# Last stage of a four-stage transformer kernel: load order, the engine that zeroes the key tiles, and the order of items within a slot

## The reference, cut to what matters

```
x = x + layer1(layer0(layernorm(x)))            # two layers, each:
h = shift_token(x); q, k, v = split(h @ wqkv)    # 8 heads of 64
q = l2norm(q) * q_scale;  k = l2norm(k) * k_scale
q, k = rotary_xpos(q, k)                         # cos and sin tables, one per position
o = softmax(8 q k^T, masked to a window of 64 back) @ v
x = x + o @ wo
h = layernorm(shift_token(x)) * g + b
a, g = split(h @ w1 + b1);  x = x + (a * gelu(g)) @ w2 + b2   # hidden width 341
```

## Time and profile before

| | us |
|---|---|
| median of 3 runs | 2061.22 |
| the profiled execution's own time | 2058.43 |
| its span on the core | 2056.5 |
| last stage, first load issued to last store issued | 1551.24 to 2050.97 |
| busy over the whole span: PE, DVE, ACT, POOL | 1762.6, 1661.3, 1602.7, 1224.6 |

### The profile page before, as it was taken

How to read it: one execution, slowest core, us unless ns; L and a number is a source line. 1 busy time by engine, 2 the same in 40 slices (tenths; PEclk the granted TensorE clock), 3 DMA queues, 4 the chain that set the end, 5 groups by cost and what they waited for, 6 DMA issues and landing times. The chain is left out here.

```text
span 2056.5 us, 37700 instructions
## 1 busy us (share of the span) xinstructions
PE 1762.6 (86%) x9830; PEld 1327.8 (65%) x9830; DVE 1661.3 (81%) x4303; ACT 1602.7 (78%) x5245; POOL 1224.6 (60%) x2106
## 2 busy tenths in 40 slices
PE   1788998899899889989989588669994999999996
PEld 0566776677677667767767456246562777777775
DVE  3799999999999999999998432768885788777784
ACT  1798999898899999999998223489971788888884
POOL 1267776777677677677777433359884555454450
PEclk8899999999999999999999699779997999999998
DMA  2222122122212222222220321012212000000000
GB/s 79 74 76 78 73 88 77 68 80 85 73 70 89 72 75 80 84 74 74 90 75 22 112 74 43 18 62 103 93 72 79 1 1 1 1 1 2 1 1 21
DMA packets 75299, 120.50 MB, mean 59 GB/s; under 512 B 10536, under 2 KB 59952, under 8 KB 67872
## 3 DMA queue, kind: packets, MB, share of 16 engines
q1 hardware_dynamic: 65920, 109.91, 15.3%
q10 hardware_dynamic: 7920, 5.60, 1.0%
q0 software_dynamic: 1248, 2.59, 0.4%
HBM read 95.44 MB, written 24.20 MB: 58 GB/s over the span
## 5 line engine op out<-in xcount | busy, mean ns | idle before, releaser
L436 ACT ACTIVATE a_prob<-a_scores,a_negmax 128x256 f32<-128x256 f32 x1536 | 706.5, 484 | 85.3 <-DVE a_negmax L538 57.9
L538 DVE TENSOR_REDUCE a_negmax<-a_scores 128x2 f32<-128x512 f32 x768 | 518.3, 675 | 43.5 <-PE a_scores L672 43.0
L684 PE MATMUL a_heads<-a_prob,a_diag 128*128 128x256 f32 x1920 | 478.2, 389 | 40.6 <-POOL a_diag L327 40.6
L327 POOL TENSOR_TENSOR a_diag<-ident,a_rowinv 128x256 f32<-128x256 f32 (+1 forms) x384 | 280.2, 735 | 248.7 <-DVE a_rowinv L592 243.5
L684 PEld LDWEIGHTS a_heads<-a_prob,a_diag 128*128 128x128 f32 x1920 | 358.3, 195 | 96.7 <-POOL a_diag L327 51.6
L672 PE MATMUL a_scores<-a_spread,a_spread 72*128 72x256 bf16 x1536 | 265.0, 276 | 92.9 <-ACT a_prob L436 53.9
L436 ACT ACTIVATION_READ_ACCUMULATOR a_prob<-a_scores,a_negmax 128x1 f32 x1536 | 330.9, 215 | 0.0
L672 PEld LDWEIGHTS a_scores<-a_spread,a_spread 72*128 72x128 bf16 x1536 | 127.6, 98 | 213.1 <-ACT a_prob L436 102.7
L1477 DVE TENSOR_TENSOR_SCAN c_state<-c_decay,c_psD 128x1024 f32<-128x1024 f32 x64 | 146.1, 2286 | 35.8 <-PE c_psD L1594 26.5
L1309 POOL TENSOR_TENSOR c_du<-c_state,c_c_row 128x1024 f32<-128x1024 f32 x64 | 151.3, 2365 | 30.3 <-DVE c_state L1477 21.2
L1933 ACT ACTIVATE d_prob<-d_psS,d_bias 128x128 f32<-128x128 f32 (+1 forms) x256 | 99.0, 396 | 35.5 <-DVE d_bias L2064 34.6
(11 more groups left out here) (291 smaller groups left out, 4111.4 us busy)
## 6 DMA issues: line engine op xcount, KB each, us to landing
a_spread<-a_split SPq DMA_DIRECT2D x48, 576.0 KB
a_spread<-a_split SPq DMA_DIRECT2D x144, 192.0 KB
a_split<-a_parts SPq DMA_DIRECT2D x48, 384.0 KB
c_c_row<-c_rows SPq DMA_DIRECT2D x32, 512.0 KB, 3.6
b_w<-in_b_w SPq DMA_DIRECT2D x1, 2816.0 KB, 14.9
a_w<-in_a_w ACTq DMA_DIRECT2D x10, 256.0 KB, 5.4
b_w<-in_b_w SPq DMA_DIRECT2D x1, 1536.0 KB, 17.9
d_wqkv<-in_d_wqkv SPq DMA_DIRECT2D x2, 768.0 KB, 5.8
```

Source lines behind the costliest of these rows:

```text
L327: g.tensor_tensor(diag[part % RING][:], ident[:].unsqueeze(1).broadcast_to([P, len(heads), P]), rowinv[part % RING][:, heads.start:heads.s ...
L436: ins = a.activation(prob[part % RING][:, c, :], psS[part % 2][:, c, :], ACT.Exp, bias=negmax[part % 2][:, c:c + 1], accum_out=rowsum[part ...
L538: v.tensor_reduce(negmax[part % 2][:, hs], psS[part % 2][:, hs, :], AX.X, ALU.max, negate=True).then_inc(s["negmax_ready"], 1)
L684: ins = p.matmul(psH[:, t, :], diag[part % RING][:, k, :], prob[part % RING][:, c, :], start=(j == 0 and k == 0), stop=(j == HG - 1 and c ...
```

## The change

Three edits. The loads are issued in another order: wqkv of layer 0, tables and both gains first, on a semaphore `first_in`, then mask and down, then the rest; PE and POOL begin on `first_in` (and `const_in`), and the rest (`weights_in`) is awaited by ACT ahead of the first exp and by PE ahead of the first turn_p. The four zero fills of kT go from DVE to POOL, two ahead of each of POOL's two first powers, and DVE waits for rot ahead of each projection instead of once. In `schedule_d` several items get other slots (shift, norm_f, turn_f, hidden and out_f one later; turn_h one later; the projections and turn_qk in other rows), and `rank` sorts a slot otherwise: hidden comes right behind exp and ahead of score, norm_f ahead of turn_p, shift behind turn_p, and turn_h, norm_o and out_f are ranked too.

```diff
--- before.py
+++ after.py
@@ -1701,22 +1701,23 @@
             place(last + 3, ("norm_o", q, t))
             place(last + 4, ("turn_o", q, t))
             place(last + 5, ("out_o", q, t))
-        place(at + 15, ("shift", q))
+        place(at + 16, ("shift", q))
         place(at + 16, ("rstd_f", q))
-        place(at + 16, ("norm_f", q))
-        place(at + 17, ("turn_f", q))
-        place(at + 22, *[("hidden", q, f) for f in range(NFD - 1)])
-        place(at + 24, ("hidden", q, NFD - 1))
-        place(at + 25, ("out_f", q))
+        place(at + 17, ("norm_f", q))
+        place(at + 18, ("turn_f", q))
+        for f, n in enumerate((23, 23, 25)):
+            place(at + n, ("hidden", q, f))
+        place(at + 26, ("out_f", q))
     for q in range(UNITS):
-        at = 8 * (q - 1)
-        place(at, ("turn_h", q))
-        for t in range(TPS):
-            for part in range(3):
-                place(at + 2 + 3 * t + part, ("project", q, t, part))
-            for part, n in enumerate(((4, 6), (6, 10))[t]):
+        at = 8 * q - 8
+        place(at + 1, ("turn_h", q))
+        for t, rows in enumerate(((1, 2, 2), (4, 5, 9))):
+            for part, n in enumerate(rows):
+                place(at + n, ("project", q, t, part))
+        for t, rows in enumerate(((5, 5), (6, 9))):
+            for part, n in enumerate(rows):
                 place(at + n, ("turn_qk", q, t, part))
-    rank = ('score', 'exp', 'shift', 'turn_o', 'turn_p', 'out_o', 'pv', 'hidden')
+    rank = ('exp', 'hidden', 'score', 'norm_f', 'turn_p', 'shift', 'turn_o', 'pv', 'out_o', 'turn_h', 'norm_o', 'out_f')
     order = []
     for n in sorted(slots):
         order += sorted(slots[n], key=lambda i: rank.index(i[0]) if i[0] in rank else len(rank))
@@ -1769,7 +1770,7 @@
         psO = ctx.enter_context(nc.psum_tensor("d_psO", [P, GRP], F32))
         psW = ctx.enter_context(nc.psum_tensor("d_psW", [P, GRP], F32))
 
-        names = ("const_in", "weights_in", "chain", "var_ready", "rstd_ready", "y_ready", "set_up",
+        names = ("const_in", "first_in", "weights_in", "chain", "var_ready", "rstd_ready", "y_ready", "set_up",
                  "rot_ready", "q_full", "q_free", "s_full", "s_free", "t_full", "t_free", "w_full", "w_free",
                  "o_full", "o_free", "square_ready", "rope_ready", "ss_ready", "inv_ready", "qk_ready", "pool_step",
                  "bias_ready", "rowinv_ready", "hn_ready",
@@ -1833,12 +1834,16 @@
         with nc.Block() as block:
             @block.sync
             def _(sp):
-                for dst, name in ((tables, "d_tables"), (mask, "d_mask"), (down, "d_down")):
+                sp.dma_start(wqkv[0][:], d["d_wqkv"][0]).then_inc(s["first_in"], 16)
+                sp.dma_start(tables[:], d["d_tables"]).then_inc(s["first_in"], 16)
+                for l in range(DEPTH):
+                    sp.dma_start(gains[l][:], d["d_gains"][l]).then_inc(s["first_in"], 16)
+                for dst, name in ((mask, "d_mask"), (down, "d_down")):
                     sp.dma_start(dst[:], d[name]).then_inc(s["const_in"], 16)
-
                 for l in range(DEPTH):
-                    for dst, name in ((wqkv, "d_wqkv"), (wo, "d_wo"), (w1, "d_w1"), (w2, "d_w2"), (cols, "d_cols"),
-                                      (gains, "d_gains")):
+                    if l:
+                        sp.dma_start(wqkv[l][:], d["d_wqkv"][l]).then_inc(s["weights_in"], 16)
+                    for dst, name in ((wo, "d_wo"), (w1, "d_w1"), (w2, "d_w2"), (cols, "d_cols")):
                         sp.dma_start(dst[l][:], d[name][l]).then_inc(s["weights_in"], 16)
 
             @block.gpsimd
@@ -1853,12 +1858,17 @@
                     g.wait_ge(s["set_up"], 2 * u + 2)
                     g.memset(prob[1][u][:, :, 0:WINDOW], 0.0).then_inc(s["set_up"], 1)
                 for k in range(2):
+                    g.wait_ge(s["set_up"], 5 + 2 * k)
+                    if k:
+                        g.wait_ge(s["rstd_ready"], k)
+                    g.memset(kT[k][P // 2:P, :, 0, :], 0.0).then_inc(s["set_up"], 1)
+                    g.wait_ge(s["set_up"], 6 + 2 * k)
+                    g.memset(kT[k][0:P // 2, :, 1, :], 0.0).then_inc(s["set_up"], 1)
                     g.wait_ge(s["var_ready"], k + 1)
                     g.tensor_tensor(mb[k]["rstd"][:], mb[k]["var"][:], minus_half[:, 0:H2], ALU.pow)\
                         .then_inc(s["rstd_ready"], 1)
-                g.wait_ge(s["set_up"], 5)
-                g.wait_ge(s["const_in"], 48)
-                g.wait_ge(s["weights_in"], DEPTH * 6 * 16)
+                g.wait_ge(s["set_up"], 9)
+                g.wait_ge(s["first_in"], (2 + DEPTH) * 16)
                 for l in range(DEPTH):
                     for k in range(4):
                         g.tensor_tensor(rot[l][:, k], tables[:, k],
@@ -1904,8 +1914,7 @@
             def _(a):
                 a.sem_inc(s["t_free"], SL)
                 a.sem_inc(s["s_free"], SL)
-                a.wait_ge(s["set_up"], 5)
-                a.wait_ge(s["weights_in"], DEPTH * 6 * 16)
+                a.wait_ge(s["set_up"], 9)
 
                 def full(it):
                     n = TI[it]
@@ -1957,6 +1966,8 @@
                             a.activation(kT[q % 2][lo, :, 0, ts], turned_in[lo], ACT.Copy)
                             a.activation(kT[q % 2][hi, :, 1, ts], turned_in[hi], ACT.Copy).then_inc(s["t_free"], 1)
                     elif kind == "exp":
+                        if it == ("exp", 0, 0):
+                            a.wait_ge(s["weights_in"], (DEPTH * 5 - 1) * 16)
                         exps(it)
                     elif kind == "turn_p":
                         t = heads(it[2])[0]
@@ -2003,12 +2014,7 @@
                                               ALU.subtract, ALU.mult)
                 chain.link(ins)
                 v.sem_inc(s["y_ready"], 1)
-                v.wait_ge(s["const_in"], 48)
-                for u in range(2):
-                    v.memset(kT[u][P // 2:P, :, 0, :], 0.0)
-                    chain.link(v.memset(kT[u][0:P // 2, :, 1, :], 0.0))
-                v.sem_inc(s["y_ready"], 1)
-                v.wait_ge(s["rot_ready"], DEPTH * 4)
+                v.wait_ge(s["const_in"], 32)
 
                 def heads3(ap):
                     return ap.rearrange("p (h e) -> p h e", e=DHD)
@@ -2019,6 +2025,7 @@
                         _, q, t, part = it
                         i = Q[it]
                         ps = psQ[i % 2]
+                        v.wait_ge(s["rot_ready"], (q // SEQS + 1) * 4)
                         v.wait_ge(s["q_full"], i + 1)
                         if part == 2:
 
@@ -2121,10 +2128,10 @@
             @block.tensor
             def _(p):
                 p.sem_inc(s["t_full"], SL)
-                p.wait_ge(s["y_ready"], 2)
-                p.wait_ge(s["const_in"], 48)
-                p.wait_ge(s["set_up"], 5)
-                p.wait_ge(s["weights_in"], DEPTH * 6 * 16)
+                p.wait_ge(s["y_ready"], 1)
+                p.wait_ge(s["const_in"], 32)
+                p.wait_ge(s["set_up"], 9)
+                p.wait_ge(s["first_in"], (2 + DEPTH) * 16)
 
 
                 def bank(it):
@@ -2172,6 +2179,8 @@
                         p.matmul(out, qT[q % 2][:, c, t * P:(t + 1) * P], kT[q % 2][:, c, :, k0:k1], start=True,
                                  stop=True).then_inc(s["s_full"], 1)
                     elif kind == "turn_p":
+                        if it == ("turn_p", 0, 0):
+                            p.wait_ge(s["weights_in"], (DEPTH * 5 - 1) * 16)
                         g = it[2]
                         t = heads(g)[0]
                         p.wait_ge(s["s_free"], S[("score", q, g)] + 1 + SL)
```

## The result

Before: 2061.18 us, median of 20 runs (2054.19 to 2068.46). After: **2073.52 us**, median of 20 (2059.61 to 2081.15). The ratio of the two is 1.0057, 95% interval 1.0041 to 1.0072: slower, by about 12 us. It lies within the range and on the side that had the largest chance, but it is twice the +6.0 of the sum.

What follows compares the result with a forecast made beforehand. PE bounded the old stage, a ring of dependencies the new repeat; -3.6 (start) - 3.6 (first unit) - 1.0 (end) + 1.1 + 13.1 (repeats) = +6.0 us on 2061.2 gave 2067.2 us, range 2050 to 2078.

Steps and rivals of the forecast that it cites:

- The repeat: Steady stretch between hidden(q,2) items on PE: 29.26 us instead of 28.17, over 12 repeats +13.1 us; chance 0.50.
- the ring: Chain of in-order and data dependencies from hidden(q,2) through PE, ACT and DVE to the next unit's: at least 29.26 us.
- PE's floor: Rival for the repeat: PE stays the bound and loses both waits, 27.17 us a repeat, total 2040; chance 0.10.
- the repeat as before: Rival: items slide past the supposed ring, the repeat stays 28.17 and only the ends change, -8.2 us, 2053; chance 0.20.
- The longer ring through psW: Rival: out_o waits for DVE's copy of shift to free psW; repeat 30.0 us, +15.7, total 2077; chance 0.12.
- The wait for rot ahead of each projection is always met: nothing.: Start step: DVE's wait for rot, now ahead of each projection, costs no time.
- nothing but the order can make a repeat longer: Bounding step: no engine gets more work, so only the order lengthens a repeat; gain at most 1.0 us a repeat.
- the first term: First unit: DVE begins the second tile's projection before the first turn_qk, saving 3.6 us, bounds 0 and 5.
- I give them half each: The two units before the 12 whole repeats, with only part of the hidden items: half a repeat's loss each, +1.1 us.
- The start: Stage start: fills on POOL and reordered loads let PE begin earlier, saving 3.6 us, bounds 1.0 and 4.5.
- My rival: Stage start: DVE's writing of y holds up POOL's fills, 1.7 us saved instead of 3.6, total 2069; chance 0.08.
- The end: Last pv and norm_o go ahead of out_f and turn_f: 2.5 us instead of 3.48, saving 1.0, bounds 0 and 2.5.

Runs made afterwards that it cites:

- the copy on and off the ring: Kernel after plus one needless 512-column DVE copy, behind the first tile's value copy (on) or norm_o (off): 2084.52 us on, 2079.83 off.
- The version above: Against before: new loads, fills on ACT, rot behind y, its wait once a layer, old order except unit 0's second tile, out_f(13), turn_f(14): 2055.36 us, ratio 0.9955.

## Why the prediction was right, and where it was not

**The repeat: right, with two legs off that cancel.** 29.26 summed, 29.22 measured with the order alone. Of the seven legs five are within 0.12 us. DVE's from the projection to the exp was 0.42 too long in the sum, and PE's from turn_p to the mark 0.55 too short. That the sum came within 0.04 us is thus partly luck. The waits named for PE (0.9 ahead of turn_p, 0.3 or more ahead of s5, none for L2112) all stand in the trace, and the copy on and off the ring shows that it is the ring that decides, more clearly still once the clock's share of the long repeats is known. PE's floor (27.17) and the repeat as before (28.17) are out. The longer ring through psW was partly right: its wait is there in each repeat (L2218, 3.2 us in 12, mostly 0.24), so the ring does close through DVE's copy of shift; its price was too high, 0.24 instead of 0.74.

**"The wait for rot ahead of each projection is always met: nothing."** This step failed. It costs 0.21 us in a new repeat and 0.14 in an old one (28.31 against 28.17), and 0.2 to 0.4 us between the fifth score and the first hidden item. Together these are some 2.8 us, a third of the 8.5 that the sum missed in the stage. So "nothing but the order can make a repeat longer" was wrong too. A met wait is no stall, but here it lengthens each hand-over behind it.

**The units ahead of the first hidden item: the term of the largest error, 5.8 us.** I had -3.6 and +1.1; measured is +3.28. Measured in two parts it is -1.95 up to unit 0's fifth score on DVE (31.40 us behind PE's start against 33.35) and +5.23 from there to the first hidden(·,2) (68.24 against 63.01). Timeline of DVE in the first unit:

```profile
1581.43 0.69 DVE L2041 TENSOR_TENSOR d_direct<-d_psQ,d_rot 128x512 f32<-128x512 f32 x1 [0.63 <-POOL d_qk L1902]
...
1592.08 0.69 DVE L2041 TENSOR_TENSOR d_direct<-d_psQ,d_rot 128x512 f32<-128x512 f32 x1 [5.78 <-ACT d_sq L1929]
```

The second tile's projection starts 13.84 us behind PE's start, where 13.8 was predicted (17.3 before), and DVE's 3.66 us of idle are gone from there. But DVE then idles 5.78 us until 1592.08, ahead of unit 1's first projection, and from 1587.70 on PE runs at 0.50. In the kernel with one rot wait a layer, where PE had 0.50 for 7.3 us less, the fifth score comes 3.24 us earlier than before (30.11), and nearly all of the predicted 3.6 is there. So the first term was near right, and some 1.3 us of it went with the clock, which differs from trace to trace.

**"I give them half each", +1.1: this is the step that failed by the most.** The same stretch behind the fifth score, at full clock in every trace, takes 67.75 us with the order alone and 68.08 with one rot wait a layer, 4.7 and 5.1 more than before. These units lack the hidden items, but may not lack the ring's other legs; that reason is mine and untested. No row stood behind the half. The version above, with the old order, has 63.03 there, and its first hidden item at 92.45, 3.9 earlier than before; some of the 3.9 may be the clock as well, at 0.50 for 12.0 us of this piece against 17.4.

**The start: 2.76 of 3.6.** The size of a fill was right (0.95 and 0.94 us, 0.91 predicted), and so was what the halves would do but for one: the loads alone cost 1.7. What was missing is who holds whom. Timeline of after:

```profile
1560.39 0.95 POOL L1864 MEMSET d_kT<- 64x1024 f32 x1
...
1560.93 0.43 DVE L69 TENSOR_SCALAR d_m_mean<-d_m_sm 128x8 f32<-128x8 f32 x1
1561.39 0.94 POOL L1866 MEMSET d_kT<- 64x1024 f32 x1
1561.40 0.97 DVE L70 TENSOR_SCALAR d_m_var<-d_m_dd 128x8 f32<-128x8 f32 x1
1561.48 5.99 DVE L2012 TENSOR_SCALAR d_y_tok<-x_tok,d_m_mean,d_m_rstd 128x128 f32<-128x128 f32 x16
...
1564.05 3.34 POOL L1874 TENSOR_TENSOR d_rot<-d_tables,d_gains 128x128 f32<-128x128 f32 x8
```

POOL's fills keep their length, and DVE's TENSOR_SCALAR of 8 elements a lane, 0.17 us elsewhere, takes 0.43 and 0.97 and ends with the fill. The same holds beside rot: y took 5.99 us for 16 tiles against 4.79 with rot behind it, and even this is 0.6 more than without fills: the first tile takes 0.95 us, until the fourth fill ends, and the ninth waits for POOL's second power. My rival had the contention, but the wrong way round (DVE holding POOL) and at the wrong instruction. The Trainium skill, "SBUF — State Buffer", section Who interferes with whom, says that a VectorE instruction in a 2-port mode and GpSimd block each other for a whole instruction: by the 0.97, which begins 0.01 us behind the fill, the trace agrees. Here the GpSimd instruction is a fill, which only writes. The BATCH_NORM_STATS2 beside the first pair of fills kept its 1.6 us.

**The end: right in kind.** From the last pv at 2044.33 to turn_o at 2046.89 it took 2.56 us, 2.5 predicted, 3.48 before. The tail as a whole bears it out between these two traces, with 1.56: both have 6.8 us at a clock of 0.50 in it, behind this place. Against other traces it can't be compared: fills alone, with the old order throughout, has 47.71 where before has 50.09, and only 2.8 us at 0.50.

**The sum.** -2.76 + 3.28 + 15.53 - 1.56 = +14.5 in the profiled executions, +12 by the medians, +6.0 predicted. The terms missed by 0.8, 5.8, 2.4 and -0.6. Of the repeats' 2.4 too many, 2.0 are the rot wait (12 x 0.17 above 29.26), the rest one repeat of 29.80.

**Open.** What lowers the clock inside the repeats of two traces (order alone, copy beside the ring) and not in the others, no run tells; each such stretch of 3.4 us cost 1.7 us. In the 29.80 of after one score on DVE (L2071, at 1782.63) starts 0.35 us late, and three other traces have one or two such starts, at other instructions; the cause is open. How the 4.7 to 5.1 us that the new order costs in the first three units are spread over its items was not taken apart either.

## What to carry to other kernels

In a software-pipelined order no engine need be the bound: follow one item through every in-order queue and back to itself, with distances between starts from the trace, and compare the sum with the busiest engine; here a copy on that ring cost its length and the same copy beside it almost nothing, and the next ring was only some tenths away. Put a wait that is needed once where it is needed once. When work is moved to an idle engine, look at what its neighbour does in the same microseconds, and price the filling of the pipeline by its own rows, not as a share of the steady state. Before a difference between two traces is put down to an edit, lay the granted clock of the same stretch side by side.

## What the runs showed of the hardware that was not expected

- A semaphore wait on DVE that is always met adds 0.11 us to each hand-over from ACT that follows it (0.80 instead of 0.69 from start to start).
- The granted clock can fall to 0.50 for 3.4 us in the middle of a steady stretch in one execution: in the order alone at 1909.50 us, with the copy beside the ring twice, each time as out_o began, and it cost 1.7 us each time. Ahead of the first hidden item, 16.7 instead of 9.4 us at 0.50 went with 1.3 us.
- A POOL fill of 64x1024 f32 holds a small DVE TENSOR_SCALAR until it ends (0.17 to 0.97 us), and POOL's TENSOR_TENSOR makes DVE's tiles of y slower (5.89 us for 16 in loads alone against 4.18 with only a power beside them; in after 5.99, of which 1.2 is rot), while POOL's fills keep their 0.95 us and its rot loses at most 0.4 us (3.75 instead of 3.34).
- The same zero fill of 64x1024 takes 0.91 us on DVE, 0.95 on POOL and 1.07 on ACT (4.29 for four): where engines are idle, it hardly matters which one takes it, and what lies beside it does.
